# A gated delta-rule decoder layer on one core: the triangular system keeps |k|² on its diagonal, decay products read PSUM, merge copies move to ScalarE

## What is computed

```
q, k, v = split(silu(conv4(x @ w_qkv)))          # q, k per key head; v per value head
q = q/|q| * 128**-0.5 ; k = k/|k|
per step t:  S = S*exp(g_t); delta_t = (v_t - k_t S)*beta_t; S = S + k_t (x) delta_t; o_t = q_t S
on = rmsnorm(o * silu(z)) * norm_w ;  y += on @ w_out
```

## Time and profile before

| | |
|---|---|
| median of 3 runs | 2510.5 us (2498.4 to 2517.4) |
| profiled execution | 2508.0 us, span 2506.2 us |
| PE busy | 2204.0 us, 88% |
| DVE busy | 1913.7 us, 76% |
| ACT busy | 1550.0 us, 62% |
| POOL busy | 789.7 us, 32% |
| granted TensorE clock, mean | 0.954 of full speed |

### The profile page before, as it was taken

The page is one execution under the profiler, slowest core; times in us unless marked ns, Lnnn a source line. Parts: engine busy times, 40 slices in busy tenths (PEclk is TensorE's granted clock), DMA queues, the critical chain, the costliest instruction groups (busy, mean ns, idle before and its releaser), DMA issues.

```text
span 2506.2 us, 47958 instructions
## 1 busy us (share of the span) xinstructions
PE 2204.0 (88%) x17852; PEld 1755.8 (70%) x17852; DVE 1913.7 (76%) x3617; ACT 1550.0 (62%) x3509; POOL 789.7 (32%) x672
## 2 busy tenths in 40 slices
PE   5448999898999989898989889899897899999998
PEld 4347887787877878787778778777785455555555
DVE  6689898988979898898989888898644755655543
ACT  4456666766666766667676667665454756566622
POOL 1433334434444344434334443442213100001000
PEclk8779999999999999999999999999998999999999
DMA  4222222221222222122122213211103000000000
GB/s 84 56 70 44 59 55 72 48 56 49 63 61 43 69 48 70 49 65 61 42 66 47 73 47 67 59 40 43 27 21 114 1 1 1 9 1 9 1 9 9
DMA packets 262341, 113.23 MB, mean 45 GB/s; under 512 B 208328, under 2 KB 239584, under 8 KB 262112
## 3 DMA queue, kind: packets, MB, share of 16 engines
q1 hardware_dynamic: 262112, 110.17, 18.3%
HBM read 82.58 MB, written 27.53 MB: 44 GB/s over the span
## 4 chain that ended last, share of the span: by engine, by line
PE 53%; DVE 33%; issue 5%; ACT 5%; DMA 2%; POOL 1%; SPq 1%; POOLq 0%; ACTq 0%; DVEq 0%
PE ps L1349 9%; DVE A L749 9%; PE ps L1481 4%; PE ps L1473 4%; PE ps L1490 4%; PE ps L1312 3%; DVE BP L1022 3%; DVE TM L818 3%; PE ps L1159 3%; DVE TM L795 3%; PE ps L1161 3%; PE ps L1160 3%; PE ps L1301 3%; PE ps L1362 2%; PE ps L1376 2%
## 5 line engine op out<-in xcount | busy, mean ns | idle before, releaser
L749 DVE SCALAR_TENSOR_TENSOR A<-ps,CW,A 128x508 f32<-128x508 f32 (+2 forms) x768 | 521.4, 735 | 16.2 <-ACT A L628 8.2
L422 POOL TENSOR_TENSOR EB<-EB,HJ 128x1024 f32<-128x1024 f32 x64 | 123.7, 1932 | 906.4 <-DMA EB<-decay_rows 906.4
L1349 PE MATMUL ps<-WO,DL 128*128 128x256 f32 x1024 | 252.6, 402 | 41.4 <-ACT DL L652 36.3
L1159 PE MATMUL ps<-XH,WH 128*128 128x512 f32 x512 | 221.9, 433 | 59.4 <-DVE A L749 47.6
L1349 PEld LDWEIGHTS ps<-WO,DL 128*128 128x128 f32 x1024 | 198.7, 200 | 84.8 <-ACT DL L652 47.6
L701 ACT ACTIVATE SC<-ps,A 128x128 f32<-128x128 f32 x512 | 141.1, 390 | 110.4 <-DVE A L1069 109.5
L1161 PE MATMUL ps<-XH,WL 128*128 128x512 f32 x512 | 208.0, 406 | 1.0 <-issue 1.0
L664 ACT ACTIVATE DL<-ps 128x512 f32<-128x512 f32 x128 | 76.6, 599 | 212.7 <-PE ps L1362 212.7
L1160 PE MATMUL ps<-XL,WH 128*128 128x512 f32 x512 | 206.7, 404 | 0.0
L1015 DVE TENSOR_TENSOR Y<-Y,ps 128x512 f32<-128x512 f32 x128 | 85.9, 682 | 106.4 <-PE ps L1349 106.3
L1159 PEld LDWEIGHTS ps<-XH,WH 128*128 128x128 f32 x512 | 100.6, 197 | 83.3 <-DVE A L749 28.1
(11 more groups left out here) (211 smaller groups left out, 5775.4 us busy)
## 6 DMA issues: line engine op xcount, KB each, us to landing
EB<-decay_rows SPq DMA_DIRECT2D x128, 256.0 KB, 4.6
x_blocks<-BP SPq DMA_DIRECT2D x256, 32.0 KB, 1.6
X<-x_blocks SPq DMA_DIRECT2D x16, 512.0 KB, 6.3
tt_blocks<-TI SPq DMA_DIRECT2D x16, 512.0 KB, 2.6
tn_blocks<-TM SPq DMA_DIRECT2D x16, 512.0 KB, 2.6
TTF<-tt_blocks SPq DMA_DIRECT2D x256, 32.0 KB, 1.9
TA<-tn_blocks SPq DMA_DIRECT2D x192, 32.0 KB, 1.9
WR<-in_L_attn_w_qkv_dram SPq DMA_DIRECT2D x32, 128.0 KB, 5.5
```

What stands on the lines that cost most here:

```text
L422: pool.tensor_tensor(ap3, ap3, at(HJ, 4 * g * 32 + 2 * hk, [[1, 2], [32, 4], [0, 128]]), ALU.add).then_inc(sem["dec"], 1)
L749: dve.scalar_tensor_tensor(acc, ps(i, 0, [[128, 4], [1, 128 - s]]), at(CW, tile * 4 + 3 - s, [[1, 1]]), acc, ALU.mult, ALU.add).then_inc(s ...
L1159: pe.matmul(out, sa, ma, start=(kt == 0), stop=False)
L1349: t = pe.matmul(ps(7 - i, b * 256, [[1, 256]]), at(DL, (4 * i + 2 * b + v) * 128, [[1, 128]]), at(WO, (k // 4 % 2) * 512 + v * 256, [[1, 2 ...
```

## The change

It does five things.

1. Normalisation is taken out of the products. The blocks hold k_s·k_t times the decay, unscaled; the diagonal of the inverse is 1/(|k|²+1e-6) in place of one. ACT's four scaled copies (L657) and the buffer `SQ` go. DVE's products (`products`) read PSUM itself, in four instructions of 512 elements each in place of two of 1024.
2. The reciprocals of |k|² of each step go to DRAM (`rk_scr`, four DMAs of 32 x 4 single elements) and come back with `load_x` as a row for each block (`RK`). `inverse` begins with two more operations: it copies RK onto the diagonal and multiplies the 2 x 2 entries by both neighbours.
3. The merge copies for U1, TTF (32) and TTF (64) go from DVE to ACT.
4. `EB` gets a third buffer, `load_rows` runs three steps ahead, and from tick 7 on `exp` is taken for two steps together in odd ticks. `squares` (the sum of squares for the norm) is cut in halves, the second of which runs in the next tick.
5. The lists of all engines are put in a new order; on PE the first half of the z projection comes ahead of u1, the transpose of `on` ahead of K K^T, and the outputs come last. On DVE the products come before the last v tap, the masked sums after it, and `pump` has room 4060 in one piece early, 500 in the middle and 2000 late.

The core of the diff:

```
-                    sp.wait_ge(sem["bp"], 2 * n + 2)
+                    sp.wait_ge(sem["bp"], 4 * n + 4)
...
+                    sp.wait_ge(sem["r2"], n + 1)
+                    for c in range(4):
+                        sp.dma_start(rk_scr[j % 2, c, 4 * g:4 * g + 4].rearrange("b s -> s b"),
+                                     at(SM, C_R2 + (n % 8) * 4, [[1, 4]], 32 * c, 32),
+                                     allow_slow_non_contiguous=True).then_inc(sem["st_rk"], 16)
...
-                    if n >= 2:
-                        sp.wait_ge(sem["bp"], 2 * (n - 2) + 2)
+                    if n >= 3:
+                        sp.wait_ge(sem["bp"], 4 * (n - 3) + 4)
...
# ScalarE, per tick
+                        act.wait_ge(sem["u1"], m + 1)
                         for i in range(2):
-                            act.wait_ge(sem["z_mm"], 2 * m + 1 + i)
-                            act.activation(z_half(m, i), ps(4 + i), ACT.Silu).then_inc(sem["z_silu"], 1)
+                            act.activation(at(U1, 0, [[1, 256]], 32 + 64 * i, 32), ps(6 + i, 0, [[1, 256]], 32 + 64 * i, 32), ACT.Copy,
+                                           scale=-1.0).then_inc(sem["u1_sb"], 1)
+                    if s3 and m:
+                        squares(m - 1, 1)
...
-                    if s1:
-                        act.wait_ge(sem["r2"], n + 1)
-                        for b in range(4):
-                            act.wait_ge(sem["kq_mm"], 2 * n + 1 + b // 2)
-                            act.activation(at(SQ, b * 256, [[1, 256]]), ps(2 + b // 2, (b % 2) * 256, [[1, 256]]), ACT.Copy,
-                                           scale=at(SM, C_R2 + b, [[1, 1]])).then_inc(sem["kqs"], 1)
...
+                    if EARLY <= n and n % 2 and n + 1 < NSTEP:
                         decay_exp(n + 1)
+                        decay_exp(n + 2)
...
# VectorE
+                dve.tensor_copy(at(TI, 0, [[33, 32]]), at(RK, 0, [[1, 32]])).then_inc(inv, 1)
...
+                def products(n, h):
+                    dve.wait_ge(sem["dec_exp"], n + 1)
+                    if n >= SLOTS:
+                        dve.wait_ge(sem["o_mm"], 2 * (n - SLOTS) + 2)
+                    dve.wait_ge(sem["kq_mm"], 2 * n + 1 + h)
+                    for v in range(2):
+                        dve.tensor_tensor(slot(n, h * 1024 + v * 256, [[512, 2], [128, 2], [1, 128]]),
+                                          ps(2 + h, 0, [[256, 2], [128, 2], [1, 128]]),
+                                          at(EB, (n % 3) * 1024 + v * 512 + h * 256, [[128, 2], [0, 2], [1, 128]]),
+                                          ALU.mult).then_inc(sem["bp"], 1)
```

More of the change, by code:

```diff
@@ L616, in _ @@
                         act.activation(at(kq_buf(n), 0, full), at(kq_buf(n), 0, full), ACT.Silu).then_inc(sem["kq_silu"], 1)
-                        if n < EARLY:
-                            kq_tap3(n + 1)
+                    if s3:
+                        act.wait_ge(sem["tt64"], m + 1)
+                        for i in range(2):
+                            act.activation(at(TTF, 32 + 64 * i, [[128, 8], [1, 32]], 64 * i, 32),
+                                           ps(6 + i, 0, [[32, 8], [1, 32]], 64 * i, 32), ACT.Copy).then_inc(sem["tt64_sb"], 1)
                     if s3:
@@ new lines, in v_proj, with on_tr @@
+                def v_proj(n, i):
+                    if n % 4 == 0 and i == 0:
+                        pe.wait_ge(sem["lo_v"], n // 4 + 1)
+                    if n + LAG3 - 1 < NSTEP:
+                        pe.wait_ge(sem["kq_conv"], 6 * (n + LAG3 - 1) + 5 + i)
+                    else:
+                        pe.wait_ge(sem["v_conv"], 6 * (n - 1) + 5 + i)
+                    proj(i, W_V + 128 * i, n % 4).then_inc(sem["v_proj"], 1)
+                def on_tr(k, i):
+                    if i == 0:
+                        pe.wait_ge(sem["on"], k + 1)
+                    if k + 1 < NSTEP:
+                        pe.wait_ge(sem["z_silu"], 2 * (k + 1) + 1 + i)
+                    elif i:
+                        pe.wait_ge(sem["delta"], 2 * NSTEP)
+                    else:
+                        pe.wait_ge(sem["x1_T"], 2)
+                    for j in range(4):
+                        t = pe.transpose(ps(4 + i, j * 128, [[1, 128]]), at(SZ, (k % 2) * 1024 + (4 * i + j) * 128, [[1, 128]]), idn)
+                    t.then_inc(sem["on_tr"], 1)
@@ new lines, in outputs @@
+                def outputs(m, i):
+                    pe.wait_ge(sem["delta"], 2 * m + 1 + i)
+                    if m:
+                        pe.wait_ge(sem["y_add"], 2 * (m - 1) + 2 - i)
+                    elif i:
+                        pe.wait_ge(sem["u2_sb"], m + 1)
+                    for j in range(4):
+                        pr = 4 * i + j
+                        t = pe.matmul(ps(6 + i, j * 128, [[1, 128]]), slot(m, pr * 256 + 128, [[1, 128]]), at(DL, pr * 128, [[1, 128]]),
+                                      start=True, stop=True)
+                    t.then_inc(sem["o_mm"], 1)
```

446 lines of the change are left out of this document (224 added, 222 removed).

## The result

The changed kernel took 2541.9 us (median of 4 runs, 2530.8 to 2555.6) against 2509.4: a ratio of 1.0135, 95% [1.0069, 1.0201]. It is slower, where 2355 had been forecast; the time is outside the range of 2305 to 2445. The profiled execution has a span of 2544.1 us.

A forecast was written before the change was run, and what follows sets the result against it. Prediction: a ring in which PE waits on DVE's order, with PE's 25.19 us a tick as floor; loop 123, tail 10 and ramp 20 us, together 153 off 2508.0, gave 2355 us, range 2305 to 2445.

The forecast's parts named there:

- SP ... so zero: SP's list: four small stores a step and the wait for r2 stay under some 10 us of room; cost zero.
- near miss of "New order": Walk of one tick in the new order: POOL's norm is ready just before PE's transpose of `on` at 9.5 us.
- POOL is done at 9.2: Same walk: squares done at 4.3 us, then POOL's norm chain of 4.9 us with gaps, ending at 9.2.
- The norm holds up PE: Rival, chance 0.07: POOL's norm takes 8.5 us, PE stands at L1335 for 3.3 us a tick; 2550 us.
- point of decision at 7.4 us: In the norm rival: length of POOL's four steps with what precedes them from which it decides, against 4.9 forecast.
- DVE's long piece: Inverse in pump's 4060 room, tick n mod 4 = 1: some 7.6 us, DVE over PE, 0.33 us a tick.
- The ramp: First ticks, rows asked for three steps ahead: 12 for tick 3, then 16 to 17 us; gain 20, between 0 and 30.
- The tail: Last seven ticks, 21.3 us each with PE busy 18.2: gain 1.4 x 8 = 10 us, between 0 and 20.
- waits for both copies: PE's waits at L1301 for DVE (56.9 us in 40 ticks) and L1349 for ACT (26.2); u2's wait forecast gone.
- Table loads: ACT, exponentials in pairs: half the loads, 1.28 us a tick less, hidden because ACT does not bound.
- Masked sums into PSUM: DVE's masked sums now write PSUM: between 0 and +0.4 us a tick, taken as 0.
- a fall by 2.2: Full loop: tick from 27.72 to 25.5 us, 2.2 us by 56 ticks = 123 us.

The follow-up runs named there:

- e4: Changed kernel with the k_scale stores in 16-byte pieces instead of single elements (scales reach RK in another order): 2434.9 us, ratio 0.9679 to before.
- e2: Changed kernel without the k_scale stores and RK loads, RK set to ones once (diagonal lacks its scale): 2406.5 us, ratio 0.9564 to before.
- e3: Changed kernel with the edits of e1 and e2 together (diagonal lacks its scale): 2385.8 us, ratio 0.9499 to before.
- e1: Changed kernel with POOL's scale_wo moved behind the norm, nothing else: 2408.3 us, ratio 0.9569 to before.
- f1: e1 with the scales transposed on PE, copied by DVE and stored as 16 pieces of 128 bytes a step: 2387.2 us, ratio 0.9514 to before.
- f2: f1 with the rooms of DVE's pump set by n mod 4: 2351.6 us, ratio 0.9377 to before.
- f4: f1 with the next k/q taps ahead of the products on DVE in the first seven ticks: 2382.4 us, ratio 0.9492 to before.
- g1: f2 and f4 together, on a third chip: 2350.7 us, ratio 0.9372 to before.
- f3: f1 with one exponential in every tick instead of two in odd ticks: 2386.9 us, ratio 0.9510 to before.
- e6: e1 with the next k/q taps ahead of the products on DVE in the first seven ticks: 2430.6 us, ratio 0.9664 to before.

## Why the prediction was wrong, by its own steps

**"SP ... so zero" failed.** The step took the stores for cheap as long as they landed in time themselves: four times 1.6 us would stay under cover. They landed late (one of them after 7.60 us, in the chain below), with RK's load 7.7 us behind them, and from 240 to 1750 us DVE waited only 1.5 us for RK, though SP itself stood 75 us in 13 times for the stores before it could issue RK's load, with other loads queued behind (1.4 us in e4, which does not tell this from the slower landings). What counted was what they do to other transfers. The decay rows went from 4.6 to 10.1 us and WO from 5.8 to 11.8, and PE had 27 to 67 us of waits that name no engine. e2 against the change prices it at 135 us, e3 against e1 at 22. The row that the step went by, x_blocks' 1.6 us, has pieces of 128 bytes; f1's stores are made of such pieces, and e3's time comes back with them. The rule of the Trainium skill (DMA: Bandwidth & Descriptors, Rules for kernel authors), one descriptor per element on a strided last dimension, was cited and then argued away. The packets of q1 agree with it: 301280 in the change and 262112 in e3, 39168 apart, of which 64 x 512 = 32768 are these stores.

**The near miss of "New order" failed, at a wait and not at a duration.** "POOL is done at 9.2" walked POOL's norm and left out what stands in its list ahead of it. `scale_wo` waits for a DMA, and in before that wait was covered: POOL stood 592.8 us for decay rows just ahead of it and so reached it 8 to 10 us after the load was asked for. The change took that cover away by its own third buffer of rows, and put the norm's user on PE ahead of K K^T. The prediction asked where POOL's old wait would go only for the ramp. e1 prices the place of `scale_wo` at 134 us with D present, e3 against e2 at 21 without. That the third buffer is what took the cover away is read from the traces of both; no run takes it back, and none asks for WO earlier in SP's list.

**The rival "The norm holds up PE" had the place and the sign, but another mechanism.** It charged 3.3 us in every tick for long POOL operations. Measured were 7.4 us on average and 10.0 at most in one tick of four, for a load. On average over the loop L504 and L506 take 2.24 and 2.33 us where L497 and L499 took 1.65 and 1.93, 1.0 us more; that alone would not have reached its point of decision at 7.4 us. It was not empty, though: in one tick of four the norm took 7.0 us in f1, and PE waited 1.7 us for it. Its 2550 agrees with 2542 by chance.

**DVE's long piece is there, and a term of it was mis-sized.** Forecast were 7.6 us for the piece and 0.33 us a tick on average. Measured were 8.9 in e3, and in f1 PE's waits for DVE come to 31.4 us in some 59 ticks, 0.5 a tick. The two L817 take 1.93 us each there instead of the 1.06 that was counted from L779. In the change itself the same operation (L824) takes 1.07, since POOL stands still just then. f2 takes back 0.59 us a tick, but most of that is PE's wait for the norm.

**The ramp (20 us forecast) brought none.** The products of the tenth step come at 225.1 us, 225.7 before, and the first output add 7.4 us later (231.3 against 223.9). Chain of the changed kernel that ended last, in the ramp:

```profile
67.10 1.28 ACT L579
70.09 1.87 DVE BP L989 x3
73.39 3.25 DVE A L788 x5
82.97 1.28 ACT L579
85.97 1.87 DVE BP L989 x3
...
106.04 7.60 DMA k_scale<-SM
113.66 6.27 DMA RK<-k_scale
```

The wait for rows is gone, but the first ticks are 18.4 and then 15 to 16 us, not 12: the taps of the next step stand behind products that wait for the exponential. Then the store and the load of the scales take 13.9 us ahead of the first inverse, where in before the store and the load of the blocks took 7.2, and from there steps are 19 to 21 us apart as before, not 16 to 17. The scales are not what keeps them so: without them (e2) the first inverse begins 1.7 us sooner, the next steps are still 18 to 20 us apart, and the first output add is 3.2 us sooner. f4, with the taps ahead of the products, is 4.6 us ahead of f1 at the first add. The rest isn't settled by a run.

**The tail (10 us) did not come.** The last seven ticks take 21.7 us each against 21.3; g1 has 21.7 as well. In f1 and f4 they take 21.0, in f2 21.7, so in g1 it is the rooms of the pump that lengthen them. Why the tail gained at most 0.3 us a tick in any of these kernels is not shown.

**What held.** The waits for both copies at L1301 and L1349 are gone. Products from PSUM take 0.68 us each, as put. Table loads are 20 and 20 instead of 40 and 40, and that is hidden (f3). DVE is busy 21.6 us a tick, 22.5 forecast. Masked sums into PSUM take 318 ns instead of 286, and the four with their reads 1.10 us instead of 0.93, within the 0 to 0.4 that was allowed; g1's ticks at PE's bound show no cost of it. The undisturbed ticks are 25.4 to 25.9 us, where 25.5 was forecast.

The account: 2547 (the profiled execution) against 2355 is 192 us. The loop has 27.79 to 28.34 us a tick instead of a fall by 2.2: 2.75 x 56 = 154. The ramp makes 27, the tail 13, and what follows the loop is 3 us shorter: 191 together. g1's 2351 close to 2355 is partly luck: its loop gains 2.81 x 56 = 157 us where 123 was forecast, and its ramp and tail give nothing of the 30 us.

## What to carry to other kernels

When a change removes a long wait from an in-order list (a list of instructions that an engine can only run one after the other), go through everything in that list that hid behind it, down to the operations that run once in four ticks: they are the next to be late. Price a small transfer by its pieces, and by what it does to the other transfers, not by its bytes or its own landing. And clear such a disturbance before testing small edits on top: the same three edits said nothing with the stores present, and two of them gave a clear answer without them.

## What the runs showed of the hardware

**Single-element stores slow the large loads.** 512 pieces of 4 bytes a tick raised the queue's share from 18.3 to 30.9% (19.0 without them, e2) and doubled the landing of 256 KB loads (4.6 to 10.1 us); 16-byte pieces gave 4.9, 128-byte pieces 4.5. The longest packet of the queue was 8.7 us, 1.8 in before. The 32 KB loads of TTF and TA, issued at another point of the tick, landed nearly as before (1.8 and 2.2 us against 1.9).

**With them come stands of PE that look like late instructions.** PE stood up to 7.4 us (e6) in the midst of a group of matmuls with nothing to wait for; with larger pieces this was gone. That the fetch is the link is read from the long packets of its queues (up to 7.4 us in the change, 1.4 before) and from the packet of q8 that ended 1.2 to 1.5 us before PE went on in all ten of the longest stands. It was not varied by itself.

**A stand of PE costs more than its length.** In the 37.0 us tick the granted clock is 0.82 on average and in the three after it 1.00; L1416 takes 3.23 us right after the stand and 1.89 in each of the next three ticks. PE had stood 1.70 us just before 1013.3 and then from 1014.7 to 1023.2; the granted clock was 0.50 (the lower level, 1.2 GHz) from 1014 to 1026 and 1.00 from 1030 on. The tick is 11 us over its neighbours for stands of 8.5 and 1.7 together; how much of the rest is clock and how much the long piece in the same tick is not separated.

**DVE and POOL operations take longer side by side.** The products of the inverse with 128x512 operands took 1.93 us each beside POOL's long ones in e3 and 1.07 on average in the change; in before L795 took 1.70 and the same step of the change, L840, 1.11. f1 and f2 differ in the rooms of the pump alone, and the same line takes, first in f1 and then in f2:

```profile
L836 DVE TENSOR_TENSOR TM<-X,TI 128x512 f32<-128x512 f32 x20 | 38.0, 1900 | 0.7
...
L836 DVE TENSOR_TENSOR TM<-X,TI 128x512 f32<-128x512 f32 x20 | 21.5, 1074 | 0.7
```

In f1 POOL is at work during these, in f2 it is not. Not every such pair slows: L806 of before took 1.06 us with POOL at work. POOL's own L516 took 3.24 us in the ticks of f1 in which the norm took 7.0, and 1.90 in the ticks after them.
